# Attention steps of a transformer layer: the fp32 products of a step in four groups instead of three, each behind a 128-column score, and the scores in one fixed turn of banks

## The reference, cut to what matters

```python
x = x + attention(layernorm(x), Wq, Wkv, Wo)     # 32 heads of 32, one shared key/value head
x = x + einsum('bsk,nk->bsn', layernorm(x), dequantized 6-bit weights) + bias

# attention
scores = einsum('bqhd,bkd->bhqk', q, k) * scale
scores = where(causal, scores + slopes * (k_position - q_position), -inf)
attn = softmax(scores, axis=-1)
out = einsum('bhqk,bkd->bqhd', attn, v)
```

## Time and profile before

| | us |
|---|---|
| median of three timed runs | 813.16 (813.12 to 813.87) |
| the profiled execution, its own time | 815.87 |
| its span, first to last instruction | 814.1 |
| PE busy in it | 802.0 |

### The profile page before, as it was taken

How to read it: one execution, slowest core, us unless ns; L and a number is a source line. 1 busy time by engine, 2 the same in 40 slices (tenths; PEclk the granted TensorE clock), 3 DMA queues, 4 the chain that set the end, 5 groups by cost and what they waited for, 6 DMA issues and landing times.

```text
span 814.1 us, 13658 instructions
## 1 busy us (share of the span) xinstructions
PE 802.0 (99%) x4624; PEld 583.3 (72%) x4624; DVE 594.1 (73%) x1594; ACT 370.3 (45%) x728; POOL 428.5 (53%) x311
## 2 busy tenths in 40 slices
PE   7999999999999999999999999999999999999998
PEld 5788888888656555656565655688887788888886
DVE  5885575657878889988888896364737768684878
ACT  2757355321566776667666665221401231041322
POOL 1000000000489988898898988431746387464465
PEclk9999999999999999999999999999999999999999
DMA  9867676566555555565467635452063613510112
GB/s 345 308 212 256 221 243 233 180 191 188 160 136 143 134 147 152 152 156 134 127 171 167 163 101 186 152 168 90 1 234 130 227 44 98 187 39 1 39 66 104
DMA packets 71534, 125.85 MB, mean 155 GB/s; under 512 B 7476, under 2 KB 16980, under 8 KB 71384
## 3 DMA queue, kind: packets, MB, share of 16 engines
q1 hardware_dynamic: 70592, 123.53, 49.5%
q10 hardware_dynamic: 872, 1.45, 0.5%
HBM read 85.61 MB, written 38.94 MB: 153 GB/s over the span
## 4 chain that ended last, share of the span: by engine, by line
PE 88%; DMA 4%; DVE 4%; issue 2%; POOL 1%; ACT 1%; ACTq 0%; SPq 0%; DVEq 0%; POOLq 0%
PE p_s L877 12%; PE p_st L906 10%; PE p_o L917 10%; PE p_o L816 7%; PE p_s L816 6%; PE p_o L930 5%; PE p_s L985 5%; PE p_s L986 5%; PE p_s L987 5%; PE p_o L818 3%; DMA inv_b<-inv_d 3%; PE p_s L818 3%; PE p_st L985 2%; PE p_st L986 2%; PE p_st L987 2%; PE p_s L1009 2%
## 5 line engine op out<-in xcount | busy, mean ns | idle before, releaser
L1496 DVE CUSTOM_DVE_ANT_0 spill<-p_s,mask 128x128 bf16<-128x128 f32 (+3 forms) x512 | 219.5, 483 | 41.6 <-PE p_s L877 41.5
L1198 ACT ACTIVATE pt<-p_st 128x512 f32<-128x512 f32 (+1 forms) x352 | 178.1, 562 | 101.8 <-PE p_st L906 101.6
L645 POOL TENSOR_SCALAR_AFFINE_SELECT pt<-pt 128x512 f32<-128x512 f32 x128 | 88.5, 704 | 234.9 <-ACT pt L1198 234.9
L877 PE MATMUL p_s<-kst,xt 98*128 98x128 f32 (+3 forms) x512 | 151.3, 343 | 0.9 <-DVE mx L1496 0.7
L906 PE MATMUL p_st<-xt,kst 100*128 100x512 f32 (+1 forms) x352 | 129.7, 388 | 0.3 <-ACT pt L1198 0.2
L877 PEld LDWEIGHTS p_s<-kst,xt 98*128 98x128 f32 x512 | 91.7, 189 | 52.7 <-DVE mx L1496 42.3
L652 POOL TENSOR_TENSOR pt<-pt 128x1536 f32<-128x1536 f32 x32 | 112.2, 3507 | 2.7
L917 PE MATMUL p_o<-pt,vst 128*32 128x512 f32 (+3 forms) x1024 | 83.0, 441 | 0.0
L658 POOL TENSOR_TENSOR pt<-pt 128x1024 f32<-128x1024 f32 x32 | 76.7, 2396 | 0.0
L906 PEld LDWEIGHTS p_st<-xt,kst 100*128 100x128 f32 x352 | 64.8, 191 | 13.7 <-issue 5.5
L816 PE MATMUL p_o<-xt,wqh 128*128 128x512 f32 x136 | 53.1, 400 | 0.8 <-DVE xt L1667 0.8
(11 more groups left out here) (212 smaller groups left out, 1621.6 us busy)
## 6 DMA issues: line engine op xcount, KB each, us to landing
xt<-qh_d SPq DMA_DIRECT2D x64, 256.0 KB
qh_d<-qh SPq DMA_DIRECT2D x32, 256.0 KB, 2.1
ql_d<-ql SPq DMA_DIRECT2D x32, 256.0 KB, 2.2
xt<-ql_d SPq DMA_DIRECT2D x32, 256.0 KB
o_d<-o_st SPq DMA_DIRECT2D x32, 256.0 KB, 2.1
ob<-o_d SPq DMA_DIRECT2D x32, 256.0 KB, 4.7
xs<-in_x_t_dram SPq DMA_DIRECT2D x28, 256.0 KB, 5.2
xin<-in_x_dram SPq DMA_DIRECT2D x14, 512.0 KB, 6.0
```

The costliest lines, as they stand in the source:

```text
L645: pool.affine_select(out=own, in_=own, compare_op=ALU.is_ge, fill=0.0, base=0, pattern=[[0, 4], [1, P]], channel_multiplier=-1).then_inc(c ...
L877: pe.matmul(scores_of(n), qst[s % 4][0:R_MAX, j, qb * P:(qb + 1) * P], kst[0:R_MAX, b * S:b * S + keys], start=True, stop=True).then_inc(s ...
L1198: act.activation(pt[s % 2][:, j:j + heads, PT_AT[kb]:PT_AT[kb] + KB_LEN[kb]], p_st[:, place(k) % 3, 0:heads * KB_LEN[kb]].rearrange("p (j ...
L1496: dve.tensor_tensor_reduce(spill[:, SPILL_AT[qb]:SPILL_AT[qb] + keys], scores_of(n), mask[:, S - keys:S], 1.0, LOWEST, ALU.add, ALU.max, m ...
```

## The change

The step's string is replaced. A stands for a head's 256-column score followed by its 128-column one, B for the 384-column one, C for the 512-column one, so that each head's scores go through banks 0, 1, 2 in strict turn, and behind each A stands one of now four groups: key block 0; key block 1; key blocks 2 and 3; the sums. Since the 256-column score is now written first (`written` gives the count of a score in the new order), it is the one that waits for the bank, and DVE waits for both of the pair before its first maximum. On DVE the transposed maxima's low part and four kinds of other work move two places or one later in the row of 16 maxima. The other engines' orders don't change.

```diff
+        def written(n):
+            return n + 1 if n < 32 or n % 4 > 1 else n + 2 if n % 4 == 0 else n
...
-                if qb != 1:
+                if qb != (1 if n < 32 else 0):
                     at_least(pe, max_done, n - qb - 4 + BANK_LAST[qb] + 1)
...
-            ORDER = "xuxuxTGxuxuxuxuGuxuxxuuxGxu"
-            GROUP = (((0,), ()), ((1, 2, 3), ()), ((), (0, 1)))
+            ORDER = "AGBuuCTAGBuuCuAGuBuCuAGuBuCu"
+            BLOCKS = {"A": (1, 0), "B": (2,), "C": (3,)}
+            GROUP = (((0,), ()), ((1,), ()), ((2, 3), ()), ((), (0, 1)))
...
-                    elif what == "x":
-                        for _ in range(2 if n % 4 == 0 else 1):
+                    elif what in BLOCKS:
+                        for qb in BLOCKS[what]:
                             if n < 4 * HEADS_ALL:
-                                score(n)
-                            n += 1
+                                score(n + 4 * heads + qb)
+                        heads += what == "C"
...
-                    dve.wait_ge(s_done, n + 2 if qb == 0 else n + 1)
+                    dve.wait_ge(s_done, max(written(n), written(n + 1)) if qb == 0 else written(n))
...
-                    if i == 3 and 0 < s < STEPS - 1:
+                    if i == 4 and 0 < s < STEPS - 1:
                         max_low(s + 1)
-                    if i == 9 and 0 <= s - 3 < HALVES:
+                    if i == 11 and 0 <= s - 3 < HALVES:
                         wo_low(s - 3)
-                    if i == 9 and s in (20, 22, 24, 26, 28):
+                    if i == 11 and s in (20, 22, 24, 26, 28):
                         o_normal((s - 20) // 2)
-                    if i == 9 and s in (21, 23, 25, 27, 29):
+                    if i == 11 and s in (21, 23, 25, 27, 29):
                         o_low((s - 21) // 2)
```

More of the change, by code:

```diff
@@ L310, in turned_max @@
         def turned_max(s):
-            return p_st[:, (TURN_AT if s > 0 else 2) % 3, 0:P]
+            return p_st[:, (TURN_AT if s > 1 else 2) % 3, 0:P]
         def wo_half(w, h):
@@ L871, in score @@
                     pe.wait_ge(k_done, 2)
-                if n % 16 == 0:
+                if written(n) % 16 == 1:
                     pe.wait_ge(q_in[s % 4], 64 * (s // 4) + 64)
-                if qb != 1:
+                if qb != (1 if n < 32 else 0):
                     at_least(pe, max_done, n - qb - 4 + BANK_LAST[qb] + 1)
@@ L881, in free_bank @@
                 before = RING * s + at - 3
-                if before % RING == TURN_AT:
+                if (s, at) == (0, 2):
+                    pe.wait_ge(ml_done, 2)
+                elif before % RING == TURN_AT:
                     at_least(pe, ml_done, min(before // RING + 2, STEPS))
@@ L934, in totals @@
                     last.then_inc(pv_done, 1)
-            ORDER = "xuxuxTGxuxuxuxuGuxuxxuuxGxu"
-            GROUP = (((0,), ()), ((1, 2, 3), ()), ((), (0, 1)))
+            ORDER = "AGBuuCTAGBuuCuAGuBuCuAGuBuCu"
+            BLOCKS = {"A": (1, 0), "B": (2,), "C": (3,)}
+            GROUP = (((0,), ()), ((1,), ()), ((2, 3), ()), ((), (0, 1)))
             FIRST_AT = {(STEPS - 2, 6): 0, (STEPS - 2, 10): 1, (STEPS - 1, 3): 2, (STEPS - 1, 6): 3, (STEPS - 1, 9): 4}
             def attend(s):
-                n, units, groups = 4 * (4 * s + AHEAD), 0, 0
+                n, units, groups, heads = 4 * (4 * s + AHEAD), 0, 0, 0
                 for what in ORDER:
```

## The result

Five timed runs of the changed kernel have a median of 817.95 us (817.84 to 818.66), beside 813.33 (813.12 to 814.09) for the kernel before on the same chip: a ratio of 1.0058, with an interval of 1.0048 to 1.0069. The forecast was 818.2. The profiled execution of the changed kernel took 817.84, with a span of 816.0.

What follows compares the result with a forecast made beforehand. PE was taken as the bound (busy 802.0 of 814.1 us). 29 steps by 0.02 (+0.6), 28 waits by 0.18 (+5.0), late places -0.5 and ends 0 gave +5.1 on 813.16: 818.2 us, range 816.4 to 819.9.

Steps and rivals of the forecast that it cites:

- The new wait for the copy: Before each block-0 group PE waits for ACT's copy of p_o: 0.18 us, 28 times, +5.0 us.
- A fourth group: In PE's step, splitting the three-block fp32 group adds no columns but one group's fixed price: +0.35 us a step.
- The pairs turned: 256-column score before the 128-column one: each pair takes 0.19 instead of 0.24 us, four times, -0.20 a step.
- DVE's waits gone: Two score weight loads a step no longer wait for DVE's maximum of the head before: -0.13 us a step.
- The late places: Occasional late steps, 0.04 us a step on average over 27, counted as half gone: -0.5 us.
- The ends: Steps 30 and 31: a fourth group and a longer copy wait against cut-up unit runs; even, 0.7 us either way.
- The clock: After step 0 the granted clock is 0.50 for 3.40 us, costing at most 1.7 us; the drop stays in.
- the clock stays up: Rival: no clock drop in steps 0 and 1, 1.6 us less, 816.6 us; chance 0.18.
- the cheap entry: Rival: entering a group behind a 128-column score costs nothing, -7.8 us, 810.4; chance 0.10.
- The copy in time: Rival: p_o's copy ends before the block-0 group needs it, 5.0 us less, 813.2, no change; chance 0.05.
- DVE's waits: Rival: scores still wait for DVE, in other places, 29 by 0.13 us, 822.0; chance 0.07.
- The pair's order: Rival: order within a pair of short scores is free, so its gain is lost: 29 by 0.15, 822.6; chance 0.05.

Runs made afterwards that it cites:

- the run with a fifth: Changed kernel with p_o's copy behind the eighth unit's exponential and the sums' group cut in two, making five groups: 823.07 us.
- the early copy: Changed kernel with ACT's copy of p_o one exponential earlier, behind the eighth unit's instead of the ninth's: 813.18 us.
- the second profile of before: Kernel before the change, no edit, run and profiled once more: 813.42 us, span 811.7.
- the first profile: Kernel before the change, no edit, the profiled execution shown ahead of the prediction: 815.87 us.
- the two copy runs: Changed kernel with ACT's copy of p_o one exponential earlier (813.18 us) or one later, behind the tenth unit's (833.09 us).
- the late copy with the store moved: Kernel before the change with p_o's copy behind the eleventh unit's exponential and SyncE's store of it behind the next query loads: 815.48 us.

## Why the prediction was right, step by step

- **The new wait for the copy**, 0.18 by 28: right in place, mechanism and size. Undoing it alone (813.18) takes back the whole loss, 0.17 a step. That it doesn't heal itself was right: one place later adds 0.49 to every step.
- **A fourth group**, +0.35: 0.33, by the run with a fifth; taking the fourth out brought new waits, so it has no price of its own. The parts fit: block 0 takes 1.00, block 1 0.78, blocks 2 and 3 0.79, the sums 1.21, and the unit behind the sums 0.34.
- **The pairs turned**, -0.20: 0.21 when turned back in the new order. The reason given, a load that hides, was incomplete: in front of a unit the same turn gives next to nothing, because the exposed load passes to the unit. The gain comes from the group behind, whose entry is paid anyway.
- **DVE's waits gone**, -0.13: worked out, not measured by itself. The step with the early copy is 9.39 and the quiet step before 9.38, so 0.33 - 0.21 leaves some -0.11 for the waits and the transpose's place together. The sign named for it, no load that waits for DVE in a quiet step, did not come: there are two a step, which lie in the shadow of a group.
- **The late places**, counted as half gone for -0.5: both are gone in the changed kernel and with the early copy (27 steps between 9.55 and 9.57, and between 9.38 and 9.40), -0.6.
- **The ends**, 0 either way by 0.7: from the last transpose to the last block-0 group 23.11 us instead of 24.23 in the second profile of before (491.47 to 515.70), and steps 0 and 1, up to the latter's transpose, 11.36 instead of 10.06. Most of both is the block-0 group, about 1.1, which has passed from one side of the transpose to the other. Together +0.2.
- **The clock**: this step failed, without harm to the forecast. I left the drop of the earlier trace rows in as part of the kernel; a second execution of before has none, nor, by their mean clock, have most others, so the changed kernel's median had nothing to gain or to lose there, and the rival "the clock stays up" subtracted 1.6 from a median that doesn't hold it. The forecast for the profiled execution, 820.9, was too high by 3.1; it carried the 2.7 us of the first profile over, of which the drop is 1.4.

The sum with the measured sizes: 29 by 0.015 (9.392 less 9.377 for a quiet step), 28 by 0.166, -0.6 and +0.2 make +4.7; measured were +4.6. That 818.2 came within 0.25 of 817.95 is in part luck: the loss was forecast 0.5 too large, and the kernel before measured 0.17 above the median from which the forecast was counted. The stated range, 816.4 to 819.9, is narrower than the bounds it was to be made of: 3.1 to 7.0 for the wait alone give 816.3 to 820.2. Of the rivals, the cheap entry is refuted by the 0.27 to 0.29 from a pair to its group: 0.12 and 0.07 for the two scores leave the 0.09 of any entry. The copy in time and DVE's waits are refuted by the two copy runs and the steps' length. The pair's order is not free before a group (819.09); before a unit it nearly is.

What stays open: why the clock fell in one of the nine runs of the late copy with the store moved, which took 819.29 (mean granted clock 0.997, the others 0.999 to 1.000), and why some steps of its profile are 9.47 to 9.49 long; and, in the first profile of before, what lies behind the 1.3 of its 2.7 us that the clock doesn't explain: 0.9 of it comes after the last transpose (321.1 us to the end instead of 320.2).

## What to carry to other kernels

When work moves within a step that repeats, count both chains to the next meeting point from one common event, and count the same place on every engine: a copy that was 2.4 us early was 0.17 late once its trigger and its reader came together, and moving it by one place in ACT's order decided between 0, 4.6 and 20 us. Before a copy, store or load is moved, look at what is queued behind its wait, on the DMA issuing engine above all, and at the thin last steps; before a subtraction on DVE is moved, what POOL is adding then, in the first step as in the others. Price a switch between kinds of products as a thing of its own, but don't take it out for its price: the pause may be what keeps the other engines ahead. And take a second profile of the kernel before calling a stretch of lower clock part of it.

## What the runs showed of the hardware

- The weight load behind a 128-column product is exposed here in either order of a pair: 0.24 + 0.23 us for the pair and a unit in one order, 0.17 + 0.31 in the other. With a group of fp32 products behind the pair the order counts: 0.27 from the pair to the group with the 128 columns last, 0.33 with them first.
- A subtraction of 128x512 on DVE that began 0.12 us into POOL's addition of 128x1536 took 3.89 us instead of 0.69 to 1.12, and ended 0.5 behind that addition. Moved two maxima earlier it took 0.69, and the kernel 813.88 us instead of 923.16. Another one took 3.69 when begun 0.30 into such an addition and 0.94 when begun 0.48 ahead of it; in the second case the addition took 3.79 us instead of 3.44.
- PE's granted clock was at 0.52 on the mean of 6.4 us after 3.6 us in which PE had worked for 0.40. At the same place in the kernel before it was at 0.50 in one profiled execution and at 1.00 in another, with PE busy for 2.42 and 2.44 of the 3 us ahead; nine of 64 timed executions of that kernel had a mean granted clock of 0.998 or less.
